# TensorE's and SyncE's batches written out, and the first steps of an expert MLP with pooling in another order

## The reference

```python
# x: (4, 1024, 512); fc1_w (2048, 512); fc2_w (384, 2048); experts_w (16, 128, 2048)
h = gelu(x @ fc1_w.T + fc1_b)
shared = h @ fc2_w.T + fc2_b
expert = h @ experts_w[indices].T + experts_b[indices]     # one expert for each batch
x = x + concatenate([shared, expert], -1)
scores = tanh(x @ W1 + b1) @ v
# a mask by prompt type (l <= j, l >= j, l != j), softmax over l, and p @ x / count
x = x + pooled
```

## Time and profile before

| | |
|---|---|
| median of 3 runs | 798.64 us (798.34 to 799.05) |
| profiled execution | 799.31 us, span 797.6 us |
| TensorE busy | 775.4 us (97%) |
| VectorE, ScalarE, GpSimd busy | 402.9, 380.0, 111.8 us |
| DMA | 177.11 MB, 222 GB/s on average |
| granted TensorE clock, mean | 0.994 |

### The profile page before, as it was taken

One profiled execution on the slowest core, in us unless ns is written; L12 is line 12 of the kernel. 1 busy time (PEld: TensorE's weight loads), 2 busy tenths in 40 slices (PEclk: granted clock), 3 DMA queues, 4 the chain that ended last, 5 costly groups with the idle time before them and its releaser, 6 DMA issues.

```text
span 797.6 us, 12351 instructions
## 1 busy us (share of the span) xinstructions
PE 775.4 (97%) x3526; PEld 633.4 (79%) x3526; DVE 402.9 (51%) x703; ACT 380.0 (48%) x641; POOL 111.8 (14%) x157
## 2 busy tenths in 40 slices
PE   7899999999999999999999999999999999999987
PEld 5688887788878888887888888888788888888866
DVE  6855576563444332754435333286254433246666
ACT  6755664453545423543445622446254552344542
POOL 3462230400000121300000022040000002204000
PEclk9999999999999999999999999999999999999998
DMA  7599898777864568867676556886596556687722
GB/s 260 175 363 319 307 355 274 233 216 216 262 200 146 173 185 270 260 210 217 220 220 204 148 192 202 279 253 189 170 303 203 166 165 209 213 284 220 224 72 106
DMA packets 130731, 177.11 MB, mean 222 GB/s; under 512 B 10064, under 2 KB 97632, under 8 KB 130656
## 3 DMA queue, kind: packets, MB, share of 16 engines
q1 hardware_dynamic: 130496, 176.20, 70.0%
q0 software_dynamic: 160, 0.01, 0.1%
HBM read 136.33 MB, written 39.85 MB: 221 GB/s over the span
## 4 chain that ended last, share of the span: by engine, by line
PE 92%; DVE 4%; DMA 1%; issue 1%; SPq 1%; ACT 0%; DVEq 0%; ACTq 0%
PE y L713 14%; PE y L715 14%; PE y L714 14%; PE hA L713 7%; PE hA L714 7%; PE hA L715 7%; PE hF L713 5%; PE hF L714 5%; PE hF L715 5%; PE j L806 2%; DVE xcl L1176 1%; PE j L814 1%; PE j L783 1%; PE j L785 1%; PE j L782 1%
## 5 line engine op out<-in xcount | busy, mean ns | idle before, releaser
L713 PE MATMUL y<-hs,w2c 128*128 128x512 f32 x512 | 202.2, 395 | 3.9 <-DVE w2c L1176 1.4
L715 PE MATMUL y<-hs,w2c 128*128 128x512 f32 x512 | 199.6, 390 | 0.0
L714 PE MATMUL y<-hs,w2c 128*128 128x512 f32 x512 | 199.3, 389 | 0.0
L713 PEld LDWEIGHTS y<-hs,w2c 128*128 128x128 f32 x512 | 96.1, 188 | 27.1 <-DVE hs L1176 4.6
L715 PEld LDWEIGHTS y<-hs,w2c 128*128 128x128 f32 x512 | 96.1, 188 | 20.5
L714 PEld LDWEIGHTS y<-hs,w2c 128*128 128x128 f32 x512 | 96.2, 188 | 19.2
L713 PE MATMUL hA<-xch,w1c 128*128 128x512 f32 x252 | 100.4, 398 | 10.0 <-DVE w1c L1176 6.2
L714 PE MATMUL hA<-xcl,w1c 128*128 128x512 f32 x252 | 98.7, 391 | 0.0
L715 PE MATMUL hA<-xch,w1c 128*128 128x512 f32 x252 | 98.6, 391 | 0.0
L703 POOL TENSOR_TENSOR x1T<-x1T,xnl 128x512 f32<-128x512 f32 x24 | 30.9, 1292 | 439.1 <-DVE x1T L1302 439.1
L971 ACT ACTIVATE hst<-hst,bcol 128x512 f32<-128x512 f32 x62 | 43.7, 721 | 87.4 <-DVE hst L1356 87.4
(11 more groups left out here) (266 smaller groups left out, 1095.5 us busy)
## 6 DMA issues: line engine op xcount, KB each, us to landing
w2c<-w2s SPq DMA_DIRECT2D x114, 384.0 KB, 3.5
w1c<-w1s SPq DMA_DIRECT2D x24, 768.0 KB, 4.5
w2c<-exs SPq DMA_DIRECT2D x114, 128.0 KB, 3.9
w1c<-w1s SPq DMA_DIRECT2D x48, 256.0 KB, 3.3
w1c<-w1s SPq DMA_DIRECT2D x24, 512.0 KB, 4.6
x1T<-in_x SPq DMA_DIRECT2D x32, 256.0 KB, 5.5
w1s<-w1c SPq DMA_DIRECT2D x8, 768.0 KB, 4.1
w2s<-w2c SPq DMA_DIRECT2D x16, 384.0 KB, 4.9
```

The source lines that it names most:

```text
L713: nc.tensor.matmul(ps, ah, bh, start=first, stop=False, skip_group_check=onto)
L714: nc.tensor.matmul(ps, ah, bl, start=False, stop=False, skip_group_check=onto)
L715: return nc.tensor.matmul(ps, al, bh, start=False, stop=last, skip_group_check=onto)
```

## The change

TensorE and SyncE no longer use the loop: the three batches are written out with constants (`run_out` on TensorE; on SyncE the same, with the four expert numbers loaded at once into a list before batch 0's first step). TensorE first waits for zeros, written by GpSimd as its first instruction, and makes 8 matmuls on them. `sum_w1(1)` and `sum_w1(2)` go from GpSimd to VectorE. T2 is made over T1's tile instead of B22's, ahead of T3. ScalarE's and VectorE's lists of the head and of pair 1 get another order. On SyncE at the last pair, the w2 loads of units 16 and 17 (`reload_w2`) come ahead of an x load, and another x load and the last two w1 stores come in phase two behind unit 19's weights.

```diff
+HEAD_TILE = {**X_TILE, T2: 0}
+HEAD_SUMS = [T1, T2, T3, T4]
+WARM = 8
@@ SyncE
+            def reload_w2(n):
+                sp.wait_ge(fc2_done, units(0, n, OC, OC))
+                sp.wait_ge(w2_out[n % W2R], 32 * (n // W2R + 1))
+                load_w2(0, n + 4)
...
                     if n % 2 == 0 and p > 0:
                         put_w1(p + 1, 1)
+                    if n == HC - 2:
+                        reload_w2(12)
...
                 if p == PAIRS - 1:
+
+                    reload_w2(13)
                     load_x(0, 0, 3)
-                    load_x(0, 0, 2)
-                    for n in (12, 13):
-                        sp.wait_ge(fc2_done, units(0, n, OC, OC))
-                        sp.wait_ge(w2_out[n % W2R], 32 * (n // W2R + 1))
-                        load_w2(0, n + 4)
-                if p > 0:
+                elif p > 0:
                     put_w1(p + 1, 2)
                     put_w1(p + 1, 3)
...
                     load_w2(b + (n + 4) // UNITS, (n + 4) % UNITS)
-                load_ex(b + 1, 0, expert_of((b + 2) % NB))
+                    if kind == "first" and u == 1:
+                        load_x(0, 0, 2)
+                        put_w1(PAIRS, 2)
+                        put_w1(PAIRS, 3)
+                load_ex(b + 1, 0, experts[(b + 2) % NB])
...
-            e = expert_of(0)
+            experts = [expert_of(0)]
             for n in range(4):
-                load_w2raw(n, e)
-            run(sp, part)
+                load_w2raw(n, experts[0])
+            for b in range(1, NB):
+                experts.append(expert_of(b))
+
+            part("first", 0)
+            for b in range(1, NB):
+                part("loop", b)
+            part("tail", NB)
@@ GpSimd
+            nc.gpsimd.memset(E4[:, 0:CT, :].bitcast(f32), 0.0).then_inc(zeros_done, 1)
             pool.dma_start(bcol[:, 0:NFIX], biases).then_inc(bias_in, 16)
...
-            sum_w1(1)
...
-            sum_w1(2)
-            link(nc.gpsimd.memset(E4[:, :, :].bitcast(f32), 0.0))
+            link(nc.gpsimd.memset(E4[:, CT:, :].bitcast(f32), 0.0))
@@ TensorE
+            pe.wait_ge(zeros_done, 1)
+            for i in range(WARM):
+                nc.tensor.matmul(yb[0][:, :], E4[:, 0, :], E4[:, 0:CT, :].rearrange("p c n -> p (c n)"), start=True, stop=True)
+            run_out(part)
@@ ScalarE, pair 1 of batch 0 (early)
                 if early:
+                    gelu_plain(2)
+                    gelu_plain(3)
                     split_head(T3, 0)
                     split_head(T3, 1)
...
                 snap(kind, b, p, P6)
                 if early:
+                    split_w2(1)
+                    split_h(b, 1)
                     split_head(T4, 0)
                     split_head(T4, 1)
-                    split_h(b, 1)
-                    split_w2(1)
...
-                if kind == "first":
+                if kind == "first" and not early:
                     split_w1(p + 1, 1)
                     split_w2(2 * p + 1)
...
                 gelu(b, p, 4)
+                if early:
+                    split_w1(p + 1, 1)
+                    split_w2(2 * p + 1)
@@ ScalarE, head
             gelu_plain(1)
+            split_h(0, 0, 1)
             split_head(T2, 0)
             split_head(T2, 1)
-            split_h(0, 0, 1)
-            gelu_plain(2)
-            gelu_plain(3)
@@ VectorE, pair 1 of batch 0
                     add(b, p, 1)
+                    split_w2(1)
+                    split_h(b, 1)
+                    add(b, p, 2)
                     split_head(T4, 0)
                     split_head(T4, 1)
-                    add(b, p, 2)
-                    split_h(b, 1)
-                    split_w2(1)
+                    add(b, p, 3)
                     split_w1(p + 1, 0)
+                    sum_w1(p + 1)
                     split_w2(2 * p)
@@ VectorE, head
+                to, a, c = {T1: (0, 1, 0), T2: (0, 3, 0), T3: (1, 3, 1), T4: (2, 2, 0)}[x_]
+                split_before = {T1: B11, T2: T1, T4: B21}.get(x_)
...
             split_head(B22, 1)
+            sum_w1(1)
             split_head(T1, 0)
             split_head(T1, 1)
             split_w1(1, 0)
             split_w1(1, 1)
-            sum_head(T3, 0)
-            sum_head(T3, 1)
             sum_head(T2, 0)
             sum_head(T2, 1)
             split_w2(0)
+            split_h(0, 0)
             split_head(T2, 0)
             split_head(T2, 1)
-            split_h(0, 0)
+            sum_head(T3, 0)
+            sum_head(T3, 1)
+            split_w1(1, 2)
+            split_w1(1, 3)
             split_head(T3, 0)
             split_head(T3, 1)
-            split_w1(1, 2)
-            split_w1(1, 3)
             sum_head(T4, 0)
             sum_head(T4, 1)
```

More of the change, by code:

```diff
@@ L283, in build @@
         out_put = [sem(f"out_put{i}") for i in range(OUTS)]
+        zeros_done = sem("zeros_done")
         const_done, mask_done = sem("const_done"), sem("mask_done")
@@ L438, in expert_of, with first_step @@
                 return sp.value_load(batch_of(tok_e, b).rearrange("(o n) -> o n", o=1), min_val=0, max_val=exp_w.shape[0] - 1)
-            def first_step(p, e, e1):
+            def reload_w2(n):
+                sp.wait_ge(fc2_done, units(0, n, OC, OC))
+                sp.wait_ge(w2_out[n % W2R], 32 * (n // W2R + 1))
+                load_w2(0, n + 4)
+            def first_step(p):
+                e, e1 = experts[0], experts[1]
                 if p + 2 <= PAIRS:
@@ L471, in first_step, with loop_step @@
                 if p == PAIRS - 1:
+                    reload_w2(13)
                     load_x(0, 0, 3)
-                    load_x(0, 0, 2)
-                    for n in (12, 13):
-                        sp.wait_ge(fc2_done, units(0, n, OC, OC))
-                        sp.wait_ge(w2_out[n % W2R], 32 * (n // W2R + 1))
-                        load_w2(0, n + 4)
-                if p > 0:
+                elif p > 0:
                     put_w1(p + 1, 2)
                     put_w1(p + 1, 3)
-            def loop_step(b, p, e1):
+            def loop_step(b, p):
+                e1 = experts[(b + 1) % NB]
                 load_w1(b, p, 0)
@@ L547, in part @@
                     return
-                e1 = expert_of((b + 1) % NB)
                 for p in range(PAIRS):
                     if kind == "first":
-                        first_step(p, e, e1)
+                        first_step(p)
                     else:
-                        loop_step(b, p, e1)
+                        loop_step(b, p)
                 second_half(kind, b)
@@ L909, in part, with run_out @@
                         job(kind, b, "u", task, pos)
-            run(pe, part)
+            def run_out(part):
+                part("first", 0)
+                for b in range(1, NB):
+                    part("loop", b)
+                part("tail", NB)
+            pe.wait_ge(zeros_done, 1)
+            for i in range(WARM):
+                nc.tensor.matmul(yb[0][:, :], E4[:, 0, :], E4[:, 0:CT, :].rearrange("p c n -> p (c n)"), start=True, stop=True)
+            run_out(part)
         @block.scalar
@@ L1134, in split_head @@
                 if x_ in (B11, B21, B22):
-                    act.wait_ge(landed[X_TILE[x_]], 16)
+                    act.wait_ge(landed[HEAD_TILE[x_]], 16)
                 else:
-                    act.wait_ge(hsum, X_SUMS.index(x_) * KH + k + 1)
-                hi(xch[:, x_, k, :], src[X_TILE[x_]]).then_inc(xhi, 1)
+                    act.wait_ge(hsum, HEAD_SUMS.index(x_) * KH + k + 1)
+                hi(xch[:, x_, k, :], src[HEAD_TILE[x_]]).then_inc(xhi, 1)
             def split_b12(k):
@@ L1388, in step @@
                 tasks(1)
-                add(b, p, 3)
+                if kind == "loop" or p > 1:
+                    add(b, p, 3)
                 if kind == "first":
@@ L1410, in part, with sum_w1 @@
                         task_part(kind, b, "u", task, pos)
+            def sum_w1(p):
+                raw = w1raw[p % 2]
+                dve.wait_ge(w1raw_in[p % 2], 16 * (p // 2 + 1))
+                nc.vector.tensor_tensor(wS[:, 0, :], raw[:, 2, :], raw[:, 3, :], ALU.add).then_inc(w1sum, 1)
+                dve.wait_ge(w1sum, 4 * p + 1 - 4)
+                nc.vector.tensor_tensor(wS[:, 1, :], wS[:, 0, :], raw[:, 0, :], ALU.subtract).then_inc(w1sum, 1)
+                dve.wait_ge(w1sum, 4 * p + 2 - 4)
+                nc.vector.tensor_tensor(wS[:, 2, :], raw[:, 1, :], wS[:, 1, :], ALU.subtract).then_inc(w1sum, 1)
+                dve.wait_ge(w1sum, 4 * p + 3 - 4)
+                nc.vector.tensor_tensor(raw[:, 2, :], raw[:, 0, :], raw[:, 2, :], ALU.subtract).then_inc(w1sum, 1)
             def split_plain(w):
@@ L1418, in split_head @@
                 dve.wait_ge(xhi, HEAD_SPLITS.index((x_, k)) + 1)
-                lo(xcl[:, x_, k, :], src[X_TILE[x_]], xch[:, x_, k, :]).then_inc(xlo, 1)
+                lo(xcl[:, x_, k, :], src[HEAD_TILE[x_]], xch[:, x_, k, :]).then_inc(xlo, 1)
```

(6 more changed lines are left out.)

## The result

The changed kernel takes 789.48 us (median of 4 runs, 789.13 to 790.28) against 798.49 in the same comparison: the ratio is 0.9882, with a 95% interval of 0.9863 to 0.9902. It is 1.2% faster, as forecast, and 0.9 us above the forecast of 788.6. The profiled execution took 789.21 us, span 787.5. Where the profiles differ by 10.1 us can be read by lining up TensorE's real matmuls (those on zeros left out) by their number in the program.

| place | before, us | after, us | difference so far | this part |
|---|---|---|---|---|
| first real matmul | 5.29 | 5.33 | +0.04 | |
| pair 2 begins | 38.81 | 35.10 | -3.71 | head -3.7 |
| matmul 400, phase one of batch 0 | 104.59 | 100.81 | -3.78 | |
| matmul 700, end of phase two | 172.85 | 166.76 | -6.09 | phase two -2.3 |
| matmul 1500, batch 1 | 348.21 | 342.14 | -6.07 | |

A forecast was written before the change was run, and what follows sets the result against it. TensorE was taken to bound the kernel, so only its gaps could be won: -3.6 (loop) - 4.2 (head) - 2.2 (phase two) = -10.0, from a median of 798.64 to 788.6 us, range 786.0 to 792.6.

The forecast's parts named there:

- The loop written out: Both turns back between TensorE's batches lose their gaps: -3.6 us, bounds -3.2 to -3.8, SyncE's writing out costed at nothing.
- The branch price: The skill's 0.11 us per compare-and-branch, by which both turns would return only 0.2 us and the whole sum be 6.6.
- The head: Before pair 2, VectorE's new order lets pair 2 begin at 34.6 instead of 38.81: 4.2 us gained, bounds 2.0 to 5.5.
- the walk: Step-by-step timing of VectorE's new list in the head: P7 at 26.0, P4 at 31.05, pair 2 at 34.6 us.
- The move itself is near nothing; what gains is the order.: In the head, weight sums on VectorE cost 1.9 us each and return about 2.2 and 2.1; reordering brings the gain.
- The zeros, 0.2 to 1.0: At the head's start, 8 matmuls on zeros raise TensorE's clock before the real matmuls, gaining 0.2 to 1.0 us alone.
- Start of phase two: In batch 0, w2 loads issued earlier remove both TensorE waits: -2.2 us, bounds -1.3 to -2.3.
- The tail, a microsecond either way: At the kernel's end, where the clock's fall comes relative to the gaps may shift the time by a microsecond.
- Slower by fetches that don't keep up: In written-out batches, 6 instruction-fetch misses of 1.7 us would cancel the gain; 805.6 with 10; chance of slower 0.03.
- Rival 2: The turn back moves to ScalarE or the branch isn't the price: 2 to 3.4 us come back, 791.3; chance 0.06.
- The numbers' loads: In the head, expert-number loads hold SyncE until ScalarE waits for raw weights, losing the head's gain: 792.8; chance 0.06.
- Rivals 1 and 3: First: head stuck on ScalarE, 790.8, chance 0.14. Other: phase two waits for something else, 790.8, chance 0.08.

The follow-up runs named there:

- kernel 3: Kernel before with TensorE's and SyncE's batches written out and expert numbers loaded once, head and phase two unchanged: 795.90 us against 799.33, ratio 0.9958.
- kernel 1: Kernel before with only TensorE's three batches written out, the other engines keeping the loop: 797.15 us against 798.57, ratio 0.9981.
- kernel 2: Changed kernel with SyncE's three batches back in a loop and expert numbers loaded in every batch: 790.99 us, ratio 0.9900.
- kernel 5: Changed kernel with TensorE's 8 matmuls on zeros made a loop of one matmul and 8 turns: 788.77 us in a single run.
- kernel 7: Changed kernel with `sum_w1(1)` and `sum_w1(2)` back on GpSimd, in the new order: 790.10 us, ratio 0.9897.
- kernel 8: Changed kernel without TensorE's wait for zeros and its 8 matmuls on them: 790.63 us, ratio 0.9887.
- kernel 6: Changed kernel with the old ScalarE and VectorE order of head and pair 1 and old T2, T4, sums staying on VectorE: 792.31 us, ratio 0.9921.
- kernel 9: Changed kernel with SyncE's old order of loads and stores at the last pair and phase two: 791.49 us, ratio 0.9907.
- kernel 4: Changed kernel, still written out, but with expert numbers read again in each of batches 1 to 3: 789.69 us, ratio 0.9886.
- kernel 10: Changed kernel with 15 more matmuls on W1's high part filling TensorE's gaps in the tail: 787.81 us, ratio 0.9855.
- kernel 11: Changed kernel with the tail's 15 filling matmuls and three more on zeros between the first product's halves: 787.79 us, ratio 0.9859.
- kernel 12: The changed kernel run again, unaltered, as the yardstick: 790.39 us, ratio 0.9886.

## Why the prediction was right, step by step

- **The loop written out, -3.6.** Measured -3.74 in the trace pairs, and 3.4 us by kernel 3. The size was right, the account of who earns it was not, and that the sum held all the same is luck in part: the change had both edits. The step "SyncE's loads run ahead of TensorE in the loop ... its writing out is costed at nothing" failed: with TensorE's alone 1.4 us are won, since SyncE's pause of 5.7 us, a turn of 3.3 and a read, then makes w1c late (kernels 1 and 2). In the profile before it had shown no wait because TensorE's turn held TensorE back by as much. I had looked for what is late next on ScalarE and stopped there; SyncE's pause between 374 and 384 us was in the trace of before too. That ScalarE's loop does not show was right (368.36).
- **The branch price** of the Trainium skill ("Advanced Engine Details and Errata", Control Flow Timing: 0.11 us, the sum 6.6) is out for this turn, whose branch stands for 5.3 us; the near branches of kernel 5 take 0.08 to 0.23 us, which is of its order.
- **The head, -4.2.** Measured -3.71 in the pair of traces, -3.9 between the middles. The walk's points came 0.5 late from the start: x landed later for the second half of the first tile (7.85 for 7.54) and VectorE's sum began at 14.09 for 13.5. At the same place kernels 7, 8 and 5 had 7.35, 7.42 and 7.45, so it is scatter of the first loads and no effect of the change. Behind it the walk held: P7 at 26.57 (26.0), P4 at 31.58 (31.05), pair 2 at 35.10 (34.6).
- **"The move itself is near nothing; what gains is the order."** Half right. Undoing the order costs 2.1 us in the traces (kernel 6), undoing the move a microsecond or more (kernel 7). The error was to compare what the sums cost in the old order with what they give back there, and not where the second one would fall in the new.
- **The zeros, 0.2 to 1.0.** Not settled by the times; the traces bear the size out where the clock rises early, which the zeros don't always bring (kernel 8). The sum has no term for them and gives no reason for that. Without them pair 2 begins at 35.77, 3.0 us ahead of the kernel before and 3.4 ahead of the middle of the old heads. So the walk's 4.2 was too large by about 1, and the early clock made up a part of it, which is luck too.
- **Start of phase two, -2.2.** Measured -2.3, and +2.6 when undone (kernel 9).
- **The tail, a microsecond either way.** -0.3 in the pair of traces. The clock is low there from 763.06 to 769.89 in the changed kernel's trace and from 765.57 to 768.98 in kernel 4's, and matmul 3400 to the end takes 32.8 and 32.3 us; over all traces without filling it is 32.0 to 33.3. That is a part of the scatter of single runs.
- **The range.** Its low end takes the 7.3 us lost in the head less the 1.6 as 5.5; it is 5.7, which would move the end from 786.0 to 785.8 and changes nothing.
- **The rivals.** Slower by fetches that don't keep up: no gap at regular distances. From matmul 1000 to 1500, in batch 1, the loop took 110.08 us and the written-out code 110.10, and there are fewer packets than before. Rival 2 (the turn's gain moves elsewhere) was real for one of the two edits alone, by SyncE and not ScalarE. The numbers' loads did hold SyncE for 5.5 us in the head (14.29 to 19.79) and nobody waited for it, as costed. Rivals 1 and 3 did not come about.

## What to carry to other kernels

When a gap of the bounding engine is taken away, ask of every queue what it did during that gap, the DMA-issuing one first: its pause may have been hidden by the very gap. Two edits that look independent can earn a part of their gain only together, so cost each with the other absent. And where the bounding engine waits for a short chain and its clock falls, work that only keeps it busy can pay though the wait stays: the matmuls behind it then run at the higher level.

## What the runs showed of the hardware that I had not expected

- A turn back over a batch's code costs TensorE 1.57 and 1.63 us idle (the kernel before), and SyncE's queue 3.0 and 3.3 (kernel 2); VectorE's takes 0.3 (the kernel before). A turn over one matmul costs nothing that shows beside 0.43 us, its branches 0.08 to 0.23 (kernel 5).
- A read of one number from DRAM into a register of SyncE takes 1.8 to 3.4 us of its queue (1.8 in the changed kernel's head, 1.9 to 2.9 in kernel 4, up to 3.4 at a batch's end in the kernel before).
- Around idle stretches of 1.07 and 2.30 us, with five tiny matmuls between them, the granted clock fell from 2.4 to 1.2 GHz, half a microsecond into the second (763.06); with 15 matmuls in these gaps it stayed (kernels 10 and 11).
- The first product began some 1.7 us later, its weights having landed late, in two of ten traces with the zeros (kernels 2 and 12), and in none of four without (kernels 1, 3, 8 and before). Whether the zeros have a part in that is open.
